# Two stacked gated 3x3 convolutions: the last image's second convolution cut 9, 6, 4, 4, 4, and seven-slot blocks for four pairs of images

## The reference

```python
def qconv_cg(x, w, theta):
    base = cin // 4
    yp = conv3x3(x[:, :base], w[:, :base])
    yr = conv3x3(x[:, base:], w[:, base:])
    return yp + sigmoid(2.0 * (yp - theta)) * yr

h = relu(bn_a(qconv_cg(x, w_a, theta_a)))
out = relu(x + bn_b(qconv_cg(h, w_b, theta_b)))
```

## Time and profile before

| | |
|---|---|
| median of three runs | 434.63 us (434.62 to 434.82) |
| span of the profiled execution | 433.1 us |
| what lies around the span, against the median | 1.5 us |
| TensorE matmuls busy | 425.9 us, 98% of the span, 7808 matmuls |
| TensorE weight loads busy | 422.3 us |
| VectorE busy | 245.6 us (57%) |
| ScalarE busy | 198.6 us (46%) |
| DMA | 27.57 MB, mean 64 GB/s |

### The profile page before, as it was taken

How to read it: one execution, slowest core, us unless ns; L and a number is a source line. 1 busy time by engine, 2 the same in 40 slices (tenths; PEclk the granted TensorE clock), 3 DMA queues, 4 the chain that set the end, 5 groups by cost and what they waited for, 6 DMA issues and landing times.

```text
span 433.1 us, 17302 instructions
## 1 busy us (share of the span) xinstructions
PE 425.9 (98%) x7808; PEld 422.3 (98%) x7808; DVE 245.6 (57%) x423; ACT 198.6 (46%) x337; POOL 30.2 (7%) x81
## 2 busy tenths in 40 slices
PE   8999999999999999999999999999999999999994
PEld 7999999999999999999999999999999999999993
DVE  6767644753764663575375375366357357436535
ACT  5765444534544653543453453354345355434322
POOL 6041000000000100000000000021000000000001
PEclk9999999999999999999999999999999999999997
DMA  7534116241615110520524161161623322012044
GB/s 151 102 78 99 27 26 125 56 92 30 125 25 101 25 28 4 99 50 3 125 55 84 37 123 30 26 123 25 122 49 61 66 51 48 4 27 50 8 93 94
DMA packets 120074, 27.57 MB, mean 64 GB/s; under 512 B 119488, under 2 KB 120000, under 8 KB 120000
## 3 DMA queue, kind: packets, MB, share of 16 engines
q1 hardware_dynamic: 117408, 25.92, 29.3%
q10 hardware_dynamic: 2272, 0.53, 0.6%
q0 software_dynamic: 320, 0.00, 0.0%
HBM read 13.60 MB, written 12.85 MB: 61 GB/s over the span
## 4 chain that ended last, share of the span: by engine, by line
PE 96%; DVE 1%; DMA 1%; issue 0%; ACT 0%; SPq 0%; DVEq 0%
PE acc L523 96%; DMA x<-in_x_dram 1%; DVE mix L822 0%; DVE rows_out L870 0%; SPq L360 0%; ACT mix L663 0%; DVE x L722 0%; ACT x_hi L625 0%; DVE natural L725 0%; DVE rows_out L912 0%; DVE rows_out L867 0%; ACT rows_out L685 0%; DVEq L821 0%; DVEq L751 0%; PE acc L550 0%
## 5 line engine op out<-in xcount | busy, mean ns | idle before, releaser
L523 PE MATMUL acc<-x_hi,w_lo 32*128 32x456 f32 (+1 forms) x1392 | 258.4, 358 | 0.0
L523 PE MATMUL acc<-x_lo,w_hi 32*128 32x456 f32 (+1 forms) x1392 | 258.3, 358 | 0.0
L523 PE MATMUL acc<-x_hi,w_hi 32*128 32x456 f32 (+1 forms) x1392 | 258.0, 358 | 0.2 <-ACT x_hi L625 0.2
L523 PE MATMUL acc<-h_hi,w_lo 32*128 32x512 f32 x1152 | 250.6, 390 | 0.0
L523 PE MATMUL acc<-h_lo,w_hi 32*128 32x512 f32 x1152 | 250.0, 389 | 0.0
L523 PE MATMUL acc<-h_hi,w_hi 32*128 32x512 f32 x1152 | 249.8, 389 | 0.0
L523 PEld LDWEIGHTS acc<-x_hi,w_hi 32*128 32x128 f32 x1392 | 217.0, 183 | 1.5 <-ACT x_hi L625 0.6
L523 PEld LDWEIGHTS acc<-x_hi,w_lo 32*128 32x128 f32 x1392 | 217.2, 183 | 0.2
L523 PEld LDWEIGHTS acc<-x_lo,w_hi 32*128 32x128 f32 x1392 | 216.9, 183 | 0.1
L523 PEld LDWEIGHTS acc<-h_lo,w_hi 32*128 32x128 f32 x1152 | 187.3, 183 | 0.4
L523 PEld LDWEIGHTS acc<-h_hi,w_lo 32*128 32x128 f32 x1152 | 186.5, 183 | 0.1
(11 more groups left out here) (77 smaller groups left out, 156.3 us busy)
## 6 DMA issues: line engine op xcount, KB each, us to landing
out_dram<-rows_out SPq DMA_DIRECT2D x95, 126.0 KB, 2.6
x<-in_x_dram SPq DMA_DIRECT2D x28, 392.0 KB, 5.5
x<-in_x_dram SPq DMA_DIRECT2D x6, 98.0 KB, 3.4
x_edge<-in_x_dram SPq DMA_DIRECT2D x4, 112.0 KB, 3.7
out_dram<-rows_out SPq DMA_DIRECT2D x3, 112.0 KB, 3.3
x<-in_x_dram SPq DMA_DIRECT2D x1, 294.0 KB, 3.9
x<-in_x_dram SPq DMA_DIRECT2D x1, 280.0 KB, 4.7
natural<-in_L_conv_w_b_dram SPq DMA_DIRECT2D x4, 36.0 KB, 3.1
```

What stands on the lines that cost most here:

```text
L523: return pe.matmul(sums(bank, blk), w[g * ROWS:(g + 1) * ROWS, tap], moving(blk, part, c, dx, g), start=(u == 0 and (alone or g == bank_gr ...
```

## The change

Four pairs of images, not two, have their first convolution in blocks of seven slots. That makes 60 "a" blocks: 32 of seven slots and 28 of eight. The last image's 27 slots of the second convolution are cut into blocks of 9, 6, 4, 4 and 4 slots, not three of 9: 46 blocks of 9, one of 6, three of 4. The end of the order is now b43, b45 (the last image's first nine slots), b44, the edge block e1, and then the 6, 4, 4 and 4 slots. These four blocks are the last round. There are 112 blocks, a multiple of four. A block of 6 slots is 342 columns, one of 4 is 228.

The last block's residual is now a slice of `x32`, and GpSimd waits for the load of the last image and not for that of the edge rows; the edge block's residual is added by `with_input` on VectorE, as the first edge block's. The helpers `b_slots`, `slots_of`, `residual_done` and `x_kept` are written for blocks of any size.

```diff
-SHORT, SHORT_PAIRS = 7, 2
+SHORT, SHORT_PAIRS = 7, 4
+THIRDS, LAST_SLOTS = (9, 9, 9), (9, 6, 4, 4, 4)
...
-    NB, NE = 3 * B, B // EDGE
-
-    second = []
+    NE = B // EDGE
+
+    b_parts, second = [], []
     for img in range(B):
-        second += [("b", 3 * img + r) for r in range(3)]
+        s0 = 1
+        for k in LAST_SLOTS if img == B - 1 else THIRDS:
+            second.append(("b", len(b_parts)))
+            b_parts.append((img, s0, k))
+            s0 += k
+        assert s0 == SLOTS
         if img == EDGE:
             second.append(("e", 0))
 
-    second[-4:] = [second[-3], second[-2], second[-4], second[-1], ("e", 1)]
+    final = len(LAST_SLOTS)
+    before_last, first_of_last = second[-final - 1], second[-final]
+    second[-final - 1:-final + 1] = [first_of_last, before_last, ("e", 1)]
...
-        return n // 3, 1 + n % 3 * BLK_B, BLK_B
+        return b_parts[n]
...
-        return second_of["b", 3 * img + 2] + 1
+        return max(second_of["b", n] for n, part in enumerate(b_parts) if part[0] == img) + 1
...
-        z_last = z[:, NA % Z_RING, 0:EDGE * W]
+        z_last = z[:, NA % Z_RING, 0:slots_of(order[-1]) * W]
...
+        def x_kept(blk):
+
+            kind, n = blk
+            if kind == "e":
+                return x_edge.rearrange("p (s w) -> p s w", w=W)
+            img, s, k = b_slots(n)
+            t = (img % X_IMGS) * XS + s
+            return x32[:, t:t + k, :]
...
-            pool.wait_ge(x_edge_landed[NE - 1], 32)
+            pool.wait_ge(x_landed[(B - 1) % X_IMGS], 32 * ((B - 1) // X_IMGS + 1))
             pool.wait_ge(out_stored[m % OUT_RING], 32 * (m // OUT_RING))
-            nc.gpsimd.tensor_tensor(out_of(m), z_last, x_edge[:, :], ALU.add).then_inc(zlast_ready, 1)
+            nc.gpsimd.tensor_tensor(out_of(m).rearrange("p (s w) -> p s w", w=W),
+                                    z_last.rearrange("p (s w) -> p s w", w=W),
+                                    x_kept(order[-1]), ALU.add).then_inc(zlast_ready, 1)
```

More of the change, by code:

```diff
@@ L127, in slots_of @@
         kind, n = blk
-        return BLK_B if kind == "b" else EDGE if kind == "e" else sum(k for img, t, k in a_slots[n])
+        return b_parts[n][2] if kind == "b" else EDGE if kind == "e" else sum(k for img, t, k in a_slots[n])
     def leading(blk):
@@ L842, in with_input @@
                     dve.wait_ge(x_edge_landed[n], 32)
[L843 to L847, removed]
+                was = x_kept(order[b])
                 to = yp_rows(b) if b in IN_BANK else out_rows_of(m)
```

## The result

The changed kernel takes 440.89 us, the median of four runs (440.03 to 441.71), against 434.62 before: the ratio is 1.0142 (95% interval 1.013 to 1.0153). It is 1.4% slower, where 434.9 us was forecast. The profiled execution has a span of 439.7 us and took 441.52.

What follows compares the result with a forecast made beforehand. TensorE's work up to S, then the store tail, were taken to bound the kernel. S +2.32, tail -2.1 and image 15's load +0.1 gave +0.3 us on 434.63: 434.9 us, range 433.8 to 436.2.

Steps and rivals of the forecast that it cites:

- Bound and split: Whole kernel: two stages count, TensorE's unbroken work to 423.28 us, then a 9.8 us tail to the span's end.
- S: End of row group 3's third turn in the last round, first block's `yr` whole: 423.28 us before the change.
- Step 1: Seven-slot blocks for two more pairs: 16 turns of 3.285 us replace 14 of 3.75, +0.06 us.
- The sign that was to show it right: Added seven-slot rounds: gates would be 3.27 to 3.29 us apart.
- Step 2: Last image's cut: one six-slot turn of 2.85 us and three four-slot turns of 2.0 replace two of 4.17, +0.51 us.
- Rival A: Four-slot turns: weight loads or instruction issue hold each at 3.3 us, giving 437.5 us; chance 0.10.
- Step 3: Last turn, 2.0 us and not 3.75: with 0.57 us more TensorE work, S moves by +2.32 us.
- Step 4: Tail behind S: six SyncE store issues to S + 5.2, landing 2.1, end 0.4; 7.7 us, 2.1 less than 9.8.
- rival C: Tail: the store queue doesn't bind, the last relu ends it, 1.0 us less, 433.9 us; chance 0.17.
- rival D: Tail: the short last round changes nothing, landing stays 3.3 us and not 2.1, giving 436.1 us; chance 0.03.
- Step 5: Image 15's load has one round less, so ScalarE waits at its split: +0.1 us, bounds 0 and 0.9.
- Step 6: Moved e1, residual slices and GpSimd's new wait for a load landing some 90 us earlier: no cost.

Runs made afterwards that it cites:

- the kernel with whole rounds: The changed kernel, same blocks reordered: while seven-slot blocks last, each round is four of them or seven, nine, seven, nine slots; 439.38 us.

## Why the prediction was wrong

*Bound and split (right).* TensorE up to S and the tail behind it were the two stages that counted, before and after.

*Step 1, seven-slot pairs at +0.06 (wrong: 2.4 us of lock more).* The price per column is right, 14.9 us for two sevens and two nines, where blocks alternate. It was read from such a round and carried to rounds of other patterns. The sign that was to show it right, gates 3.27 to 3.29 us apart, failed. ScalarE's gates after:

```profile
149.05 0.68 ACT L682 ACTIVATE mix<-acc,gate_bias 128x504 f32<-128x504 f32 x1 [2.90 <-PE acc L542]
...
152.47 0.59 ACT L682 ACTIVATE mix<-acc,gate_bias 128x392 f32<-128x392 f32 x1 [2.73 <-PE acc L542]
...
160.25 0.68 ACT L682 ACTIVATE mix<-acc,gate_bias 128x504 f32<-128x504 f32 x1 [1.26 <-PE acc L542]
...
164.08 0.59 ACT L682 ACTIVATE mix<-acc,gate_bias 128x392 f32<-128x392 f32 x1 [3.14 <-PE acc L542]
```

The gates of two seven-slot blocks follow the ones before by 3.42 and 3.83 us. That is not row group 0's turns alone: by its matmul records these two took 3.32 and 3.27 us. In 446 of the changed kernel's 448 turns the signal that a turn has ended came within 0.05 us of the latest end among all matmuls up to it in the program, and so up to 0.7 us behind its own end. So the distance of two gates is a turn only where the row group is equally far ahead at both. The time was lost elsewhere in these rounds, as in round 8: 0.73 and 0.83 us in the turns of row groups 0 and 1 at a21 and a22. The pattern itself was harmless with eight slots, round 8 before: 0.05; there an eight-slot turn is only 0.44 us shorter than a nine-slot one.

*Step 2, small turns (right).* A row group's matmuls of 228 columns are 113 ns apart (median), 18 of them 2.03 us; 342 columns, 157 ns, 2.83 us. Rival A is out. By the Trainium skill's rule on weight loads (TensorE: Matmul & The Clock Gate, Part 3) a four-slot turn would have been 3.9 us, by the prediction's estimate; the trace does not agree.

*Step 3, S moves by the sum of the turns (wrong by what steps 1 and 6 left out, and by 0.2 us of lock in the last round).*

*Step 4, the tail (right).* First store at S + 1.8, six SyncE issues 0.66 us apart, with no gap, the sixth at 437.1, S + 5.1, the last relu done at 436.19, 0.9 us before it, landing 2.1 us, 7.7 in all. The sixth issue waited for the queue and not for its relu, so rival C is out, and rival D by the landing. Two side figures of this step were wrong without harm: in the kernel before, issues in a row start 0.64 to 0.69 us apart and not 0.69 throughout, and the lower bound of 0.43 us an issue is in no row (five of them would give S + 4.0, not S + 4.6).

*Step 5, image 15's load (right).* ScalarE stood 4.07 us at the split:

```profile
348.54 0.63 ACT L644 ACTIVATE x_hi<-x 128x504 fp32r<-128x504 f32 x1 [4.07 <-DMA x<-in_x_dram]
```

Round 22 is 0.18 us over its price here, and from -0.01 to 0.42 in the other runs with this order; 0.1 was forecast, with 0.9 as the bound. The same wait for an earlier image, in round 19 (0.22 us), was not in the sum.

*Step 6, "At nothing: the moved e1" (wrong: 3.85 us).* This is the step that failed most. e1's place stayed 107, and that looked like no change; but what counts is its distance to the last first-convolution block and in which round that block is finished. In the kernel before the last "a" block closed round 24; with two "a" blocks more and two "b" blocks more it opens round 25. The forecast followed the new waits of GpSimd and SyncE, and not the old one of TensorE whose other end had moved. It cost 2.3 us as a break, and in the profiled execution 1.6 us more of half clock behind it. None of the four rivals named this wait or the lock of step 1.

Not settled: why a row group runs at most three steps ahead. No edit tried it; the records show only that it does, and that the late matmuls stand at that distance.

## What to carry to other kernels

A price per unit holds for the pattern that it was read from. Where several queues share one order of issue, ask of each new pattern how far their steps run apart, and look at the idle time of the weight loads, which shows it when no wait does. Of a block that keeps its place, ask whether what it reads has moved; and if a break appears in TensorE, look at the granted clock behind it.

## What was not expected of the hardware

A stop of TensorE of 1.67 us was followed by half clock for about 3 us in the changed kernel's profiled execution, and one of 1.64 us by none in that of the kernel with whole rounds. That the same differs between runs of one kernel, up to 2.2 us apart, is read from their times and mean granted clocks; only one run of each was profiled. With one row group of four kept busy through the stop the profiled clock stayed at 1.00, and the four runs lay within 0.44 us. The Trainium skill (TensorE: Matmul & The Clock Gate, Part 3) has matmuls start and end in the order of the program. By that, a round of two sevens and two nines, in which at each step some row group is at a nine, would take four long turns, 16.7 us; it takes 14.9, so starts do run apart here, by up to three steps, while the signals of ended turns did come in the program's order (step 1). Where the order of turns asked for more than three steps, up to 1.3 us of a round was lost (round 13 of the kernel with six short pairs).
